# Router logits of a graph layer with the router weights as the stationary operand, four quarters of the array side by side, and a changed routing order

## The chip, the cores and the metric

The kernel runs on one core of a Trainium2 chip. The metric is the device time of one execution in microseconds (us). In this text PE is TensorE (PEld its weight loads), DVE is VectorE, ACT is ScalarE, POOL is GpSimd and SP is the queue that issues most DMAs. An fp32 product is shown in the profile as two records ("passes"); a product of the rounded type fp32r, and a transpose, as one.

## The reference, cut to what matters

Everything is float32, 384 tokens of 1024 features. A graph attention (16 heads, edge mask) and a linear attention with a gated feed-forward net are added to the input; the sum is normalised and goes through a mixture of eight experts, of which each token takes one:

```python
x = x + gnn(xn, ...) + mix(xn, ...)
t = layernorm(x)                              # 384 x 1024
logits = t @ switch_w + switch_b              # 384 x 8
route_prob = softmax(logits)
routes = argmax(route_prob)
for e in range(8):                            # w1[e] 1024 x 512, w2[e] 512 x 1024
    y = gelu(t @ w1[e] + b1[e]) @ w2[e] + b2[e]
    out = where(routes == e, y, out)
x = x + out * max(route_prob)
```

The change is in how `t @ switch_w` is formed, and in the order of what stands around it.

## The kernel before, in words

Each engine has its own program, written out in order, and they meet at semaphores. Tokens are in three tiles t of 128 rows, features in eight groups k of 128. Most matrix products are made of three fp32r products of high and low parts. The last stage before the experts goes like this:

- The output projection (`project`, L1770) adds the attention to `tok`. Its second half is done tile by tile; after a tile DVE adds it up (`projected`, L1282 to L1287) and subtracts the mean (`centred`, L1309), which gives x2[t]. POOL makes 1/sigma (`rstd`, L515).
- PE transposes x2[t] (L1791) into two PSUM banks, ACT copies them to `x2t[t]` (L856; for the third tile DVE copies one of the two, L1424), and scales x2[t] into its high part (L864 to L867, semaphore `x2_hi`). DVE then makes the low part (`split_x2`, L1297, semaphore `x2_split`).
- `logits(t)` (L1799): for each k the 128x128 block of `x2t[t]` is the stationary operand and the 8 columns of `swt` move through; 8 fp32 products, added up in PSUM. Tiles 0 and 1 come in a row, before the transposes of tile 2, which come before the logits of tile 2.
- DVE's `choices` (L1384 to L1401) finds the expert of each token as a row of zeros and a one (`hot_r`). PE counts how many tokens of each expert stand before each token (L1850 to L1852 for tiles 0 and 1, L1880 and L1881 for tile 2), and DVE's `places` (L1410 to L1417) makes of it a matrix `place[t]` of 128 tokens by 512 slots.
- `gather` (L1865): with x2's high and low parts as stationary operands and `place[t]` moving, PE sorts the tokens by expert: 8 k, 2 parts, 3 tiles, 48 fp32r products of 512 columns. ACT copies the results. Then the experts' products follow (L1917), for two experts at a time, each in one half of the array's columns, with their weights in a ring of 30 buffers that SP fills as they are read.

Of the kernel before, what the change touches and what calls it, by code (L numbers as in the profile page):

```python
# [18 lines left out]
ALU = mybir.AluOpType  # L19
ACT = mybir.ActivationFunctionType  # L20
F32 = mybir.dt.float32
F32R = mybir.dt.float32r
I32 = mybir.dt.int32
AX_X = mybir.AxisListType.X

P = 128
N = 384
NT = N // P
D = 1024
KT = D // P  # L30
# [9 lines left out]
EXPERTS = 8  # L40
# [17 lines left out]
C_EXP = C_SLOT + OVER * EXPERTS  # L58
C_IOTA = C_EXP + 1
# [17 lines left out]
EARLY = 5  # L77
# [70 lines left out]
def graph_layer(nc, x, rowb, cols, consts, later, src_rows, dst_rows, src_cols, dst_cols, type_cols,  # L148
                type_weights, w_stream, w_experts, switch_w, b12, out):
    with ExitStack() as ctx:  # L150
        def sb(name, shape, dt=F32):
            return ctx.enter_context(nc.sbuf_tensor(name, shape, dt))

        def sem(name):
            return ctx.enter_context(nc.semaphore(name))
# [24 lines left out]
        with nc.sbuf_tensor("place_ab", [P, NT * N], F32R) as place_ab:  # L180
            pass
        maskb = sb("maskb", [P, NT, N])
        with nc.sbuf_tensor("edges_a", [P, 2, N], I32) as edges_a:
            pass
        qp = sb("qp", [P, 2, N], F32R)
# [48 lines left out]
        vt = row_buf[:, 0:N]  # L234
        qp_row, kp_row = qp[:].rearrange("p a b -> p (a b)"), kp[:].rearrange("p a b -> p (a b)")
        tri_r, place_late = qp_row[:, 0:2 * P], qp_row[:, 0:NT * SLOT].rearrange("p (t n) -> p t n", t=NT)
        ident = cst[:, C_ID:C_ID + P]
        tri = cst[:, C_TRI:C_TRI + P]
        ones = cst[:, C_ONE:C_ONE + P]
# [73 lines left out]
            sem("pos_done"))  # L313
        tri_set, hots_set = sem("tri_set"), sem("hots_set")
        x2t_half = sem("x2t_half")
        place_done, got_ready, got_done = sem("place_done"), sem("got_ready"), sem("got_done")
        blk_in = [sem(f"blk_in{h}") for h in range(len(HOMES))]
        blk_read = sem("blk_read")
# [40 lines left out]
        def x2t_banks(t):  # L359

            return (3, 4) if t == 1 else (0, 2)

        def logit_bank(t):

            return 1 if t < 2 else 0
# [272 lines left out]
        def _(act):  # L638
# [220 lines left out]
            def split_x2(t):  # L859

                act.wait_ge(rstd_done, 3 * NT + t + 1)
                r = rs[:, t, 1:2]
                if t < 2:
                    nc.scalar.activation(pt_row[:, t * D:(t + 1) * D], x2[t], ACT.Identity, scale=r).then_inc(x2_hi, 1)  # L864
                else:
                    nc.scalar.activation(pt_row[:, 2 * D:2 * D + 2 * P], x2[t][:, 0:2 * P], ACT.Identity, scale=r)
                    nc.scalar.activation(vp_row, x2[t][:, 2 * P:D], ACT.Identity, scale=r).then_inc(x2_hi, 1)  # L867
# [6 lines left out]
                                         bias=rt[:, R_NMAX, t:t + 1], accum_out=rt[:, R_SUM, t:t + 1])\  # L874
                        .then_inc(lexp_done, 1)

            for t in range(NT):
                x2t_copy(t)
                split_x2(t)
            act.wait_ge(lmax_done, 1)  # L880
            exponentials(0, 2)
            act.wait_ge(lmax_done, 2)
# [38 lines left out]
        def _(dve):  # L921
# [368 lines left out]
            def split_x2(t):  # L1290

                dve.wait_ge(x2_hi, t + 1)
                dve.wait_ge(x2t_ready, t + 1)

                def rest(dst, value, hi):

                    return nc.vector.scalar_tensor_tensor(out=dst, in0=value, scalar=rs[:, t, 1:2],  # L1297
                                                          in1=hi.bitcast(F32), op0=ALU.mult, op1=ALU.subtract)

                if t < 2:  # L1300
                    rest(x2_lo[t], x2[t], pt_row[:, t * D:(t + 1) * D]).then_inc(x2_split, 1)
                else:
                    rest(x2_lo[t][:, 0:2 * P], x2[t][:, 0:2 * P], pt_row[:, 2 * D:2 * D + 2 * P])
                    rest(x2_lo[t][:, 2 * P:D], x2[t][:, 2 * P:D], vp_row).then_inc(x2_split, 1)
# [24 lines left out]
            for first in (0, 32):  # L1329
                rows = slice(first, first + EXPERTS)  # L1330
                ins = nc.vector.tensor_copy(kp_row[rows, 0:EXPERTS * SLOT].rearrange("p (s n) -> p s n", n=SLOT),
                                            slote[rows, 2, 0:EXPERTS].unsqueeze(2).to_broadcast([EXPERTS, EXPERTS, SLOT]))
            ins.then_inc(hots_set, 1)
            for b in range(HALF // P):
                nc.vector.tensor_scalar(iota[:, b * P:(b + 1) * P], cst[:, C_IOTA:C_IOTA + P], float(b * P), None,
                                        ALU.add)
# [16 lines left out]
            projected(1, 1)  # L1353
            centred(1)
            split_x2(0)
            split_x2(1)
            projected(1, 2)
            centred(2)

# [44 lines left out]
            def places(first, last, counted):  # L1404

                ts = range(first, last)
                dve.wait_ge(hot_done, counted)
                dve.wait_ge(count_ready, counted)
                for t in ts:
                    ins = nc.vector.scalar_tensor_tensor(out=of_tile(R_RANK, t), in0=count_of(t), scalar=1.0,  # L1410
                                                         in1=hot_of(t).bitcast(F32), op0=ALU.mult, op1=ALU.mult,
                                                         accum_out=seen[:, t:t + 1])
                then(ins)
                nc.vector.tensor_scalar(valid[:, first:last], seen[:, first:last], float(SLOT), None, ALU.is_lt)
                then(nc.vector.tensor_tensor(near[:, first:last], seen[:, first:last], own[:, first:last], ALU.add))
                for t in ts:
                    nc.vector.tensor_scalar(place[t], iota[:], near[:, t:t + 1], valid[:, t:t + 1],  # L1417
                                            ALU.is_equal, ALU.mult).then_inc(place_done, 1)

            dve.wait_ge(route_in, 32)  # L1420
            dve.wait_ge(logits_ready, 1)
            choices(0, 2)
            dve.wait_ge(x2t_ready, NT)
            nc.vector.tensor_copy(x2t[2][:, HALF:D], ps[:, x2t_banks(2)[1], :]).then_inc(x2t_half, 1)  # L1424
            places(0, 2, 1)
            dve.wait_ge(logits_ready, 2)
            choices(2, NT)
            places(2, NT, 2)
# [125 lines left out]
        def _(pe):  # L1554
# [239 lines left out]

            def logits(t):

                pe.wait_ge(x2t_copied, t + 1)
                for k in range(KT):
                    ins = nc.tensor.matmul(ps[:, logit_bank(t), t * EXPERTS:(t + 1) * EXPERTS],  # L1799
                                           x2t[t][:, k * P:(k + 1) * P],  # L1800
                                           swt[:, k, :], start=(k == 0), stop=(k == KT - 1))
                return ins

            pe.wait_ge(s_max, HEADS - 1)
            pe.wait_ge(out_lo, PAIRS - 2)
# [26 lines left out]
            project(1, 2, 3).then_inc(w_started, 1)  # L1832
            q_no.add(RING)

            pe.wait_ge(route_in, 32)
            logits(0)
            logits(1).then_inc(logits_ready, 1)
            transpose_x2(2)
# [11 lines left out]
            nc.tensor.matmul(count_of(0), tri_m, hot_of(0), start=True, stop=True)  # L1850
            nc.tensor.matmul(count_of(1), ones_m, hot_of(0), start=True, stop=False)
            nc.tensor.matmul(count_of(1), tri_m, hot_of(1), start=False, stop=True).then_inc(count_ready, 1)  # L1852
            pe.wait_ge(x2t_copied, NT)
            pe.wait_ge(x2t_half, 1)
            logits(2).then_inc(logits_ready, 1)

            def x2_part(part, t, k):
# [10 lines left out]
                    ins.then_inc(got_ready, 1)  # L1868

            pe.wait_ge(wo_sum, 2 * NT)  # L1870
            pe.wait_ge(x2_split, 2)
            pe.wait_ge(place_done, 2)
            for part in range(2):
                gather(0, part, 0, 2)
            for u in range(2):
                both = ps[:, 1, (NT + 2) * EXPERTS:(NT + 4) * EXPERTS].rearrange("p (t e) -> p t e", e=EXPERTS)
                nc.tensor.matmul(both, ones_m, hot_of(u).unsqueeze(1).to_broadcast([P, 2, EXPERTS]),
# [1 line left out]
            pe.wait_ge(hot_done, 2)  # L1879
            nc.tensor.matmul(count_of(2), tri_m, hot_of(2), start=False, stop=False)  # L1880
            nc.tensor.matmul(count_of(3), ones_m, hot_of(2), start=False, stop=True).then_inc(count_ready, 1)  # L1881
            for k in range(1, EARLY):
                for part in range(2):
                    gather(k, part, 0, 2)
            pe.wait_ge(x2_hi, NT)
            pe.wait_ge(place_done, NT)
            for k in range(EARLY):
# [208 lines left out]
```

## Time and profile before

| | us |
|---|---|
| median of 3 runs | 587.9 |
| lowest, highest | 587.04, 591.64 |
| profiled execution | 588.1 |
| its span, first to last instruction | 586.3 |

| engine | busy us | share of the span | instructions |
|---|---|---|---|
| PE | 557.9 | 95% | 3048 |
| PEld | 478.7 | 82% | 3048 |
| DVE | 379.5 | 65% | 743 |
| ACT | 239.0 | 41% | 387 |
| POOL | 147.1 | 25% | 161 |

Around the span lie 1.8 us in which no instruction runs. Busy time of PE counts a product that is in the array, whether it fills it or not, and at whichever of its two clocks it runs; so the share says that PE has nearly always work, not that it works at its peak. The stage that the change touches is the stretch from 483 to 507 us of the span.

### The profile page before, as it was taken

The page shows a single profiled execution, that of the slowest core. Times are in us where ns is not written, and L with a number is a line of the kernel's source. Part 1 is how long each engine was busy: PE and PEld are TensorE (multiplying, and loading weights), DVE is VectorE, ACT ScalarE, POOL GpSimd, SP SyncE. Part 2 cuts the span into 40 slices and gives each one's busy share as a digit, 9 for nine tenths or more (in the row PEclk, how much of TensorE's full clock was granted, in tenths as well). Part 3 has the DMA queues.
Part 4 walks back from the last instruction along what each step waited for, and adds up shares of the span by engine and source line. Part 5 has one row for each costly group of instructions (what it writes and reads, how often), then busy time and mean ns, then how long its engine had stood idle before and what let it go on. Part 6 is the DMA issues. An engine that isn't in the chain of part 4 may idle for free.

```text
span 586.3 us, 8511 instructions
## 1 busy us (share of the span) xinstructions
PE 557.9 (95%) x3048; PEld 478.7 (82%) x3048; DVE 379.5 (65%) x743; ACT 239.0 (41%) x387; POOL 147.1 (25%) x161
## 2 busy tenths in 40 slices
PE   3989999999999999999999999999998999999995
PEld 3989997897999999999979999999997888633321
DVE  6688887755777447673558889888979776200114
ACT  3646553410233434344326665676477321320000
POOL 5627665751176500080000001001002010000020
PEclk9999999999999999999999999999998996999998
DMA  8655657530263554448532226325459686199943
GB/s 304 212 143 193 163 175 235 148 107 1 71 190 109 187 180 140 149 148 285 149 82 103 72 72 153 98 72 143 143 182 315 248 325 266 63 387 412 411 161 110
DMA packets 33777, 104.18 MB, mean 178 GB/s; under 512 B 5424, under 2 KB 9712, under 8 KB 33744
## 3 DMA queue, kind: packets, MB, share of 16 engines
q1 hardware_dynamic: 28224, 89.95, 44.5%
q0 software_dynamic: 5376, 13.29, 8.7%
q10 hardware_dynamic: 144, 0.52, 0.3%
q8 instruction: 17, 0.28, 0.2%
q14 instruction: 16, 0.13, 0.1%
HBM read 96.58 MB, written 5.60 MB: 174 GB/s over the span
## 4 chain that ended last, share of the span: by engine, by line
PE 83%; DVE 7%; ACT 3%; DMA 2%; issue 2%; POOL 1%; DVEq 0%; SPq 0%; ACTq 0%
PE ps L1577 42%; PE ps L1917 10%; PE ps L1770 6%; PE ps L1591 5%; PE ps L1724 3%; PE ps L1714 3%; DVE wsp L933 2%; PE ps L1865 2%; PE ps L1699 2%; PE ps L1661 2%; PE ps L1642 2%; PE ps L1734 2%; DMA tw<-in_type_weights 1%; PE ps L1799 1%; DMA tok<-in_x 1%
## 5 line engine op out<-in xcount | busy, mean ns | idle before, releaser
L1577 PE MATMUL ps<-big,wsp 128*128 128x384 f32 x1656 | 295.6, 337 | 3.6 <-DVE wsp L933 2.8
L1577 PEld LDWEIGHTS ps<-big,wsp 128*128 128x128 f32 x1656 | 286.0, 188 | 8.1 <-issue 5.6
L933 DVE TENSOR_TENSOR wsp<-raw,wsp 128x1024 fp32r<-128x1024 f32 x85 | 111.0, 1311 | 30.6 <-ACT wsp L650 29.7
L650 ACT ACTIVATE wsp<-raw 128x1024 fp32r<-128x1024 f32 x83 | 87.0, 1052 | 32.9 <-PE ps L1591 12.9
L559 POOL DMA_INDIRECT edge_table<-ef,eidx x48 | 55.5, 1155 | 34.5 <-DMA edge_table<-ef,eidx 22.5
L657 ACT ACTIVATE big<-ps,bias 128x384 f32 x24 | 14.0, 582 | 80.8 <-PE ps L1577 80.8
L1917 PE MATMUL ps<-blocks 128*64 128x512 f32 x192 | 43.8, 599 | 0.0
L944 DVE SCALAR_TENSOR_TENSOR big<-ps,bias,big 128x384 f32 (+1 forms) x24 | 14.8, 617 | 34.1 <-ACT big L657 33.5
L774 ACT ACTIVATE work<-work,snm 128x384 f32<-128x384 f32 x48 | 28.9, 604 | 16.1 <-DVE snm L1200 16.1
L1591 PE MATMUL ps<-wsp,big 128*128 128x512 f32 x144 | 33.1, 391 | 0.4 <-DVE wsp L933 0.4
L1917 PEld LDWEIGHTS ps<-blocks 128*64 128x64 f32 x192 | 12.7, 136 | 23.8 <-issue 23.8
L1591 PEld LDWEIGHTS ps<-wsp,big 128*128 128x128 f32 x144 | 27.0, 188 | 6.3 <-DVE wsp L933 0.8
L596 POOL DMA_DIRECT2D tok<-rowbuf x3 | 2.8, 934 | 96.5 <-ACT tok L801 96.5
L515 POOL TENSOR_SCALAR rs<-mv 128x1 f32<-128x1 f32 x12 | 6.1, 506 | 81.7 <-DVE mv L952 47.5
L1482 DVE COPY maskb<-ps 128x512 f32<-128x512 f32 x4 | 2.8, 692 | 34.8 <-PE ps L1917 34.8
L1196 DVE CUSTOM_DVE_ANT_0 work<-ps,maskb 128x384 f32<-128x384 f32 x48 | 24.1, 553 | 1.6 <-issue 1.6
L933 DVE TENSOR_TENSOR pt<-ps,pt 128x1152 fp32r<-128x1152 f32 x16 | 21.7, 1357 | 1.4 <-ACT pt L782 1.3
L1482 DVE COPY row_buf<-ps 128x512 f32<-128x512 f32 x4 | 2.8, 691 | 30.5 <-PE ps L1917 30.5
L1009 DVE SCALAR_TENSOR_TENSOR work<-codes,ef,maskb 128x384 f32<-128x384 int32 (+2 forms) x48 | 22.1, 510 | 0.0
L1724 PE MATMUL ps<-pt,vp 128*128 128x384 f32 x96 | 20.2, 345 | 1.1 <-DVE pt L933 0.7
L1770 PE MATMUL ps<-wsp,big 128*128 128x512 f32 x72 | 18.9, 421 | 1.8 <-DVE snm L1200 1.8
L782 ACT ACTIVATE pt<-ps 128x1152 fp32r<-128x1152 f32 x16 | 18.1, 1134 | 3.7 <-PE ps L1714 3.5
(242 smaller groups left out, 722.7 us busy)
## 6 DMA issues: line engine op xcount, KB each, us to landing
raw<-in_w_stream SPq DMA_DIRECT2D x85, 512.0 KB, 3.6
blocks<-in_w_experts SPq DMA_DIRECT2D x64, 512.0 KB, 9.2
rowbuf<-in_rowb POOLq DMA_DIRECT2D x6, 512.0 KB, 6.0
raw_x<-in_w_stream SPq DMA_DIRECT2D x4, 512.0 KB, 7.3
slot_y<-rowbuf POOLq DMA_DIRECT2D x7, 256.0 KB, 5.8
tok<-in_x SPq DMA_DIRECT2D x3, 512.0 KB, 4.0
edges_a<-in_src_rows SPq DMA_DIRECT2D x8, 192.0 KB, 4.3
edges_a<-in_dst_rows SPq DMA_DIRECT2D x8, 192.0 KB, 5.4
```

Source lines behind the costliest of these rows:

```text
L559: pool.indirect_dma_start(out=table, out_offset=bass.IndirectOffsetOnAxis(ap=eidx[:, c:c + 1], axis=0), in_=ef[:, 3, c:c + 1], in_offset=N ...
L650: nc.scalar.activation(wsp[:, 0, slot, :], raw[:, slot, :], ACT.Copy).then_inc(w_hi, 1)
L774: nc.scalar.activation(probs[:, s, t, :], probs[:, s, t, :], ACT.Exp, bias=snm[:, s, t:t + 1], scale=DH ** -0.5, accum_out=ssum[:, s, t:t ...
L782: nc.scalar.activation(pt[:, 0, :, :], ps[:, b:b + 3, 0:N], ACT.Copy).then_inc(pt_hi, 1)
L933: return nc.vector.tensor_tensor(dst, value, hi.bitcast(F32), ALU.subtract)
L1009: ins = nc.vector.scalar_tensor_tensor(out=into[k], in0=codes[buf][:, k * P:N], scalar=ef[:, 0, bass.ds(c + k, 1)], in1=maskb[:, k, k * P: ...
L1196: ins = nc.vector.tensor_tensor_reduce(out=probs[:, s, t, :], in0=ps[:, 2 + 3 * s + t, 0:N], in1=maskb[:, t, :], scale=1.0, scalar=3.0 * N ...
L1577: ins = nc.tensor.matmul(ps[:, bank, 0:N], wsp[:, a, slot, k * P:(k + 1) * P], moving[:, b, k, :], start=(k == 0 and n == 0), stop=(k == K ...
L1591: ins = nc.tensor.matmul(ps[:, banks + t, :], stationary[:, b, k, t * P:(t + 1) * P], wsp[:, a, slot, kk * HALF:(kk + 1) * HALF], start=(k ...
L1724: ins = nc.tensor.matmul(ps[:, bank, 0:N], vp[:, mt, s, :], pt[:, b, mt, :], start=(mt == 0 and b == 0), stop=(mt == NT - 1 and b == 1))
L1770: ins = nc.tensor.matmul(ps[:, 2 + 3 * h + t, :], feat[0][:, b, k, t * P:(t + 1) * P], split_of(slot_of(Q_WO + h * RING + j), a)[:, kk * H ...
L1917: ins = nc.tensor.matmul(ps[s * SLOT:(s + 1) * SLOT, bank, :], stationary(k, s), rows[s][:, kk * HALF:(kk + 1) * HALF], start=False, stop= ...
```

## The change

The roles in the product are swapped. `switch_w` is spread out to 32 columns per k (8 weights, 24 zeros) in a tile `swt_wide`, which is now the stationary operand, and the 128 columns of `x2t[t]` move. Since it fills a quarter of the array's columns, four k are put side by side, each in its quarter, so that PSUM gets the four partial sums of k = g and k = 4 + g in 32 partitions each (`partial_logits`). ACT copies the 128x128 result to SBUF (`l_copy`), and one more product with a matrix `fold` (128x8, ones where the row's expert is the column) adds the four quarters and turns the result to tokens by experts (`logits`). DVE builds `swt_wide` and `fold` once, ahead of `iota`.

Around it the order changes: DVE's low part of tile 1 (`split_x2(1)`) comes after `places(0, 2)`. On ACT the copies of the logits stand after `split_x2(1)` and, for tile 2, ahead of `split_x2(2)`, behind a wait for the first logits. PE's early gathers take first the high parts of k = 0 to 4 and then the low ones, three of the high ones ahead of the counts of tile 2.

```diff
+        l_rows = [routing[:, (2 + n) * P:(3 + n) * P] for n in range(2)]
+        swt_wide = routing[:, 2 * N + 4 * P:2 * N + 6 * P].rearrange("p (k e) -> p k e", e=32)
+            def l_copy(t):
+                act.wait_ge(l_ready, t + 1)
+                nc.scalar.activation(l_rows[t % 2], ps[:, l_bank(t), 0:P], ACT.Copy).then_inc(l_copied, 1)
-            for t in range(NT):
+            for t in range(2):
                 x2t_copy(t)
                 split_x2(t)
+            for t in range(2):
+                l_copy(t)
+            x2t_copy(2)
+            act.wait_ge(logits_ready, 1)
+            l_copy(2)
+            split_x2(2)
...
+            then(nc.vector.memset(swt_wide, 0.0))
+            dve.wait_ge(route_in, 32)
+            nc.vector.tensor_copy(swt_wide[:, :, 0:EXPERTS], swt[:])
+            groups = cst[:, C_IOTA:C_IOTA + P].rearrange("p (g n) -> p g n", g=4)[:, :, 0:EXPERTS]
+            then(nc.vector.tensor_scalar(fold_of.rearrange("p (g e) -> p g e", g=4), groups, cst[:, C_EXP:C_EXP + 1],
+                                         None, ALU.is_equal))
+            nc.vector.reduce_sum(fold, fold_of.rearrange("p (g e) -> p e g", g=4), AX_X).then_inc(swt_set, 1)
...
             split_x2(0)
-            split_x2(1)
             projected(1, 2)
...
             places(0, 2, 1)
+            split_x2(1)
             dve.wait_ge(logits_ready, 2)
...
             def logits(t):
+                pe.wait_ge(l_copied, t + 1)
+                return nc.tensor.matmul(ps[:, logit_bank(t), t * EXPERTS:(t + 1) * EXPERTS], l_rows[t % 2], fold,
+                                        start=True, stop=True)
+            def partial_logits(t):
                 pe.wait_ge(x2t_copied, t + 1)
-                for k in range(KT):
-                    ins = nc.tensor.matmul(ps[:, logit_bank(t), t * EXPERTS:(t + 1) * EXPERTS],
-                                           x2t[t][:, k * P:(k + 1) * P],
-                                           swt[:, k, :], start=(k == 0), stop=(k == KT - 1))
-                return ins
+                for r in range(2):
+                    for g in range(4):
+                        k = 4 * r + g
+                        ins = nc.tensor.matmul(ps[32 * g:32 * (g + 1), l_bank(t), 0:P], swt_wide[:, k, :],
+                                               x2t[t][:, k * P:(k + 1) * P], start=(r == 0), stop=(r == 1))
+                ins.then_inc(l_ready, 1)
...
-            pe.wait_ge(route_in, 32)
+            pe.wait_ge(swt_set, 1)
+            partial_logits(0)
+            partial_logits(1)
             logits(0)
             logits(1).then_inc(logits_ready, 1)
             transpose_x2(2)
...
-            pe.wait_ge(x2t_copied, NT)
             pe.wait_ge(x2t_half, 1)
+            partial_logits(2)
             logits(2).then_inc(logits_ready, 1)
...
-            pe.wait_ge(x2_split, 2)
+            pe.wait_ge(x2_hi, 2)
             pe.wait_ge(place_done, 2)
-            for part in range(2):
-                gather(0, part, 0, 2)
+            for k in range(3):
+                gather(k, 0, 0, 2)
...
-            for k in range(1, EARLY):
-                for part in range(2):
-                    gather(k, part, 0, 2)
+            for k in range(3, EARLY):
+                gather(k, 0, 0, 2)
+            pe.wait_ge(x2_split, 2)
+            for k in range(EARLY):
+                gather(k, 1, 0, 2)
```

How PE's program reads from the logits of tile 1 to the first gather, before (a name ahead of the arrow is the PSUM tensor, behind it stand the moving and the stationary operand; the shape is that of the result):

```order
L1799 MATMUL ps<-swt,maskb 128x8 [waits x2t_copied]
L1799 MATMUL ps<-swt,maskb 128x8 x7
L1791 MATMUL ps<-cst,work 128x128 [waits x2_done]
L1791 MATMUL ps<-cst,work 128x128 x7
L1850 MATMUL ps<-hot_r,qp 128x8 [waits hot_done,tri_set]
L1851 MATMUL ps<-hot_r,qp 128x8
L1852 MATMUL ps<-hot_r,qp 128x8
L1799 MATMUL ps<-swt,row_buf 128x8 [waits x2t_copied,x2t_half]
L1799 MATMUL ps<-swt,row_buf 128x8 x7
L1865 MATMUL ps<-place_ab,pt 128x512 [waits place_done,x2_split,wo_sum]
```

And PE's program of the change at the same place (`routing` holds `swt_wide`, `l_rows` and `fold`):

```order
L1834 MATMUL ps<-maskb,routing 32x128 [waits x2t_copied]
L1834 MATMUL ps<-maskb,routing 32x128 x7
L1825 MATMUL ps<-routing 128x8 [waits l_copied] x2
L1818 MATMUL ps<-cst,work 128x128 [waits x2_done]
L1818 MATMUL ps<-cst,work 128x128 x7
L1886 MATMUL ps<-hot_r,qp 128x8 [waits hot_done,tri_set]
L1887 MATMUL ps<-hot_r,qp 128x8
L1888 MATMUL ps<-hot_r,qp 128x8
L1834 MATMUL ps<-row_buf,routing 32x128 [waits x2t_copied,x2t_half]
L1834 MATMUL ps<-row_buf,routing 32x128 x7
L1825 MATMUL ps<-routing 128x8 [waits l_copied]
L1901 MATMUL ps<-place_ab,pt 128x512 [waits place_done,x2_hi,wo_sum]
```

The groups of eight products stand where they stood (that of tile 0 is right ahead of these rows in both); behind tiles 0 and 1 come two products, behind tile 2 one, that wait for ACT's copies, and the first gather no longer waits for `x2_split`.

ACT's program in the same stretch, of the change. Before, the three rows of L890 were not there:

```order
L866 ACTIVATE maskb<-ps 128x512 [waits x2t_ready]
L866 ACTIVATE maskb<-ps 128x512
L874 ACTIVATE pt<-rowbuf,rs 128x1024 [waits rstd_done]
L890 ACTIVATE routing<-ps 128x128 [waits l_ready] x2
L866 ACTIVATE row_buf<-ps 128x512 [waits x2t_ready]
L890 ACTIVATE routing<-ps 128x128 [waits l_ready,logits_ready]
L876 ACTIVATE pt<-work,rs 128x256 [waits rstd_done]
L877 ACTIVATE vp<-work,rs 128x768
L883 ACTIVATE rt<-rt 128x8 [waits lmax_done]
```

## Rows read from the trace of the kernel before

**Rows 1.** The chain that ended last, 483 to 515: start us, us, what.
```profile
483.47 3.48 PE ps L1799 x32
...
487.04 0.37 DVE rt L1384 x2
...
488.82 0.35 PE ps L1850
...
489.38 0.21 PE ps L1852
489.59 3.42 PE ps L1799 x16
493.01 1.91 PE ps L1865 x4
...
495.57 11.27 PE ps L1865 x44
...
507.16 0.23 PE ps L1925
507.39 7.02 PE ps L1917 x32
514.41 0.44 PE ps L1925
```

**Rows 2.** Windows, PE alone: us, PE busy (x), PEclk, DMA share, GB/s.
```profile
443.50:444.00 0.50, 0.50 (x2) 0.50 1.01 385
...
446.50:447.00 0.50, 0.50 (x3) 0.82 1.05 426
...
487.60:487.80 0.20, 0.20 (x3) 0.61 1.07 430
...
497.80:498.00 0.20, 0.20 (x2) 0.79 0.00 0
```

**Rows 3.** Timeline of PE: start, us, line, op, out<-in, count [idle before <-releaser].
```profile
442.92 5.98 PE L1770 MATMUL ps<-wsp,big 128*128 128x512 f32 x18 [1.83 <-DVE snm L1200]
```

**Rows 4.** Timeline of DVE, 456 to 495.
```profile
456.77 0.70 DVE L1319 MEMSET kp<- 128x768 f32 x1
...
466.82 0.69 DVE L1282 TENSOR_TENSOR tok<-tok,ps 128x512 f32<-128x512 f32 x1 [1.13 <-PE ps L1770]
...
482.91 1.28 DVE L1297 SCALAR_TENSOR_TENSOR x_lo_ab<-rowbuf,rs,pt 128x1024 fp32r<-128x1024 f32 x1 [2.35 <-ACT pt L864]
484.11 0.68 DVE L1282 TENSOR_TENSOR tok<-tok,ps 128x512 f32<-128x512 f32 x1
...
485.80 0.75 DVE L1309 TENSOR_SCALAR work<-tok,mv 128x1024 f32<-128x1024 f32 x1
487.04 0.36 DVE L1384 SCALAR_TENSOR_TENSOR rt<-ps,rs,sbias 128x8 f32<-128x8 f32 x2 [0.49 <-PE ps L1799]
...
488.65 0.68 DVE L1424 COPY row_buf<-ps 128x512 f32<-128x512 f32 x1
489.71 0.17 DVE L1410 SCALAR_TENSOR_TENSOR rt<-ps,hot_r 128x8 f32<-128x8 f32 x1 [0.37 <-PE ps L1852]
...
490.27 1.00 DVE L1417 TENSOR_SCALAR place_ab<-iota,rt 128x512 fp32r<-128x512 f32 x2
493.05 0.23 DVE L1384 SCALAR_TENSOR_TENSOR rt<-ps,rs,sbias 128x8 f32<-128x8 f32 x1 [1.78 <-PE ps L1799]
...
494.03 0.23 DVE L1398 TENSOR_SCALAR hot_r<-rt 128x8 fp32r<-128x8 f32 x1
```

**Rows 5.** Timeline of ACT, 461 to 490.
```profile
461.30 0.49 ACT L790 ACTIVATE low_rows<-ps 64x384 f32<-64x384 f32 x1 [3.14 <-PE ps L1724]
...
488.00 0.60 ACT L856 ACTIVATE row_buf<-ps 128x512 f32<-128x512 f32 x1 [5.13 <-PE ps L1791]
...
489.72 0.29 ACT L873 ACTIVATE rt<-rt 128x8 f32<-128x8 f32 x1
```

**Rows 6.** Timeline of PE, 571 to 575.
```profile
571.45 2.84 PE L1958 MATMUL ps<-row_buf,iota 128*128 128x512 f32 x6
```

More of the change, by code:

```diff
@@ L182, in graph_layer @@
         maskb = sb("maskb", [P, NT, N])
+        with nc.sbuf_tensor("routing", [P, 4 * N], F32) as routing:
+            pass
         with nc.sbuf_tensor("edges_a", [P, 2, N], I32) as edges_a:
@@ L236, in graph_layer @@
         tri_r, place_late = qp_row[:, 0:2 * P], qp_row[:, 0:NT * SLOT].rearrange("p (t n) -> p t n", t=NT)
+        l_rows = [routing[:, (2 + n) * P:(3 + n) * P] for n in range(2)]
+        fold_of, fold = routing[:, 4 * P:4 * P + 4 * EXPERTS], routing[:, 4 * P + 4 * EXPERTS:4 * P + 5 * EXPERTS]
+        swt_wide = routing[:, 2 * N + 4 * P:2 * N + 6 * P].rearrange("p (k e) -> p k e", e=32)
         ident = cst[:, C_ID:C_ID + P]
@@ L315, in graph_layer @@
         x2t_half = sem("x2t_half")
+        swt_set, l_ready, l_copied = sem("swt_set"), sem("l_ready"), sem("l_copied")
         place_done, got_ready, got_done = sem("place_done"), sem("got_ready"), sem("got_done")
@@ L361, in x2t_banks, with l_bank @@
             return (3, 4) if t == 1 else (0, 2)
+        def l_bank(t):
+            return 4 if t == 1 else 2
         def logit_bank(t):
@@ L1418, in places @@
                                             ALU.is_equal, ALU.mult).then_inc(place_done, 1)
-            dve.wait_ge(route_in, 32)
             dve.wait_ge(logits_ready, 1)
```

## The prediction

> **What bounds the kernel now.** I first read the shares of busy time: PE has work in 95% of the span, so a gain must shorten what PE does or how long it waits. Then the chain of waits around the change [rows 1]. It runs from the projection into the logits of tiles 0 and 1 (483.47, 3.48 us), over DVE's choice of experts (487.04) to PE's counts (488.82), through the logits of tile 2 (489.59, 3.42 us) into the gathers (493.01 to 506.84) and straight on into the experts' products. So the whole stretch is on the path, and what the gathers' end moves, the end of the kernel moves: behind it the view of waits shows none of PE on a load, and the later loads are released by PE's own reading. Last I read the granted clock [rows 2]. It is at 2.4 GHz up to 487.68 (0.61 over 0.2 us), at 1.2 GHz until 497.88 (0.79), and 2.4 GHz again. It had done the same before: 1.2 GHz by 443.5, back at 446.68 (0.82 over 0.5 us). That is why sixteen passes of logits take 3.42 us for tile 2 and only 1.74 us each for tiles 0 and 1.
>
> Gathering at full clock is 11.4 us of work: 4.87 us at half clock (493.01 to 497.88) count as 2.43, and 8.96 us follow.
>
> **The change, part by part.**
>
> *The products.* A logits pass of before takes 3.48/32 = 0.109 us though only 8 columns move; its stationary operand is 128 wide. Of the new passes (the same number, two for each of eight products) each moves 128 columns against 32 stationary ones. No row shows such a pass. The nearest are the experts' products, two halves side by side: 7.02/32 = 0.219 us a pass of 512 columns [rows 1], where the same type across the full array takes 2.84/6 = 0.47 [rows 6]. So there the array does two at once. A quarter of the columns moved gives 0.219/4 = 0.055 us a pass. That is also what I take with four quarters: the two passes of one product need the same quarter and must follow each other, and if products start in order, only the second pass of one and the first of the next can overlap, however many quarters there are. The ends are 0.027 (all four at once) and 0.109 (nothing overlaps). Going from full width to parts of the array and back costs a little: a full product behind full ones takes 0.23 us in the chain, behind halves 0.44 [rows 1], so 0.21 us each time. There are two such trips, and I double that at half clock.
>
> The Trainium skill, "TensorE: Matmul & The Clock Gate", Part 1, has a rule against this: if the sequencer's microcode decodes them, matmuls come no faster than one in about 62 ns. The closest passes in my rows are these 0.109 us apart, so no run here shows whether it holds; with 0.062 the first 32 passes would take 0.2 us more and the result would be an estimated 0.2 us later.
>
> *The copy.* ACT has nothing to do between its work for tile 1 (done at 482.9) and 488.00 [rows 5]. A copy of 64x384 from PSUM takes 0.49 us, 128x512 0.60, and the smallest operation 0.29; so 128x128 is between 0.29 and 0.49, and I take 0.30, since by the first two 128 columns cost 0.11 and 128 instead of 384 leave 0.27. The copy of tile 0 lies under the passes of tile 1; that of tile 1 is on the path, with some 0.05 us for each hand-over.
>
> *The folding product.* Two passes behind a wait: as for L1850 and L1852, 0.35 and 0.21 at half clock [rows 1], I take 0.25 + 0.11 at full clock and 0.1 for the hand-over.
>
> *Tiles 0 and 1.* 483.47 + 0.21 + 32 x 0.055 = 485.44; copy done 485.8; logits at 486.25; DVE starts at 486.3. Before it started at 487.04: 0.7 us earlier. DVE itself must be free: its chain `projected` to `centred` of tile 2 ran from 484.11 to 486.55, held up by the low part of tile 1 that started at 482.91 and took 1.28 [rows 4]. That low part is moved away, so the chain starts at 483.55, ends at 486.0, and is no wait, nor is it one for the transposes of tile 2, which follow at 486.25. Without this move DVE would still be busy until 486.55, and the gain would be 0.5.
>
> *Tile 2.* The counts come 0.7 us earlier, at 488.12, and end at 488.89. DVE's half copy of x2t (488.65 to 489.33) moves along and is in time. Passes at half clock: 2 x 0.21 + 16 x 0.11 = 2.18 gives 491.07; ACT's copy, for which only a wait for the first logits stands ahead, 491.45; folding 0.1 + 0.35 + 0.21 gives 492.1. Before: 493.01. So the gathers can begin 0.9 us earlier.
>
> *What stands behind the new waits.* On ACT the high part of tile 2 now waits for that copy and starts at 491.45; it and the low part are wanted only behind the 20 early gathers, which alone take over 4.5 us. On DVE `places(0, 2)` starts at 489.0 (0.7 before 489.71) and ends at 490.57; then comes the low part of tile 1, 1.28 us, until 491.85, and the logits of tile 2 at 492.15 are not kept waiting. The margin is 0.3 us: with quicker logits DVE becomes the next wait. The new order of the gathers covers the 1.2 us in which DVE chooses for tile 2 (493.05 to 494.2 before): at half clock six products of 1.91/4 = 0.48 us [rows 1]. The gathers' number is the same, 48.
>
> *Setting up.* Four DVE operations ahead of `iota`: a fill of 128x256 (0.70 us for 128x768, so 0.25) and three small ones, together about 0.9 us. They are covered by 1.13 us in which DVE waited for PE at 466.82 [rows 4]; if they overran, 2.35 us of waiting at 482.91 would take it. No DMA, SP or POOL instruction is moved.
>
> *The clock.* Gathers from 492.1 run at half clock until it comes back. In the first stall the dense products began at 442.92 [rows 3] and the clock rose 3.76 us later; in the second the gathers began at 493.01 and it rose 4.87 later. I take the middle, 4.3 us: at 496.4, 2.15 of the 11.4 us are done, and 9.25 remain: 505.65 instead of 506.84, 1.2 us earlier. The ends 3.76 and 4.87 give 1.5 and 0.9.
>
> The sum is against the profiled execution: 588.1 - 1.2 = 586.9. That execution is 0.2 above the median of the runs, 587.9; I make no correction for it.
>
> **The rivals.**
>
> *The clock comes back in the middle of this.* The new passes move 128 columns, not 8. If they count as dense work, the 3.76 to 4.87 us run from 489.1, and the clock rises near 493.4. The gathers have then done 0.65 us and need 10.75 more: 504.15, a gain of 2.7, 585.4. For it speaks that the fall at 487.68 came after 3.4 us of nearly nothing but 8-column products and transposes; against it the waits that now stand between the groups.
>
> *All four quarters at once.* 0.027 us a pass saves 0.9 us in the first 32 passes and 0.9 in the next 16: a further 1.8, 585.1. The Trainium skill, "TensorEngine Tiling (Array Packing)", Overview, gives up to 4x for 32 columns. The halves' two-fold overlap agrees with that rule and with products starting in order alike.
>
> *The clock never falls.* Then the logits of tile 2 would be there at 490.6, but DVE is in the low part of tile 1 until 491.8 and chooses until 493.0; PE stands for 0.8 us behind its three early gathers. It ends at 502.9: 584.2. Idle PE time grows with the change, which speaks against it.
>
> *Slower: the passes do not overlap in quarters.* The one mechanism is the spacing of the 32-column passes. At 0.109 us nothing is saved in the products, and copies, folding products and trips come on top: DVE starts at 488.0 instead of 487.04, the counts end at 490.5, the 16 passes take 3.9 us, the gathers begin at 495.5. They end at 509.05, 2.2 us later: 590.3. It decides from a spacing of about 0.074 (64 units of spacing, counting tile 2 double, for 1.2 us). The halves speak against it; that only halves, never quarters, are seen here speaks for it.
>
> *No gain to be seen.* Hand-overs and trips cost 0.3 us more each time and eat it: 588.0.
>
> **How the numbers follow.** Forecast 0.38, clock back early 0.20, four at once 0.08, never falls 0.04, no gain 0.13, slower 0.17. The predicted time is the likeliest case's, 586.9. The range 584.8 to 589.3 takes in the first three and no gain, and of the slower case the spacings up to about 0.09; 584.2 and the full 590.3 are out, some 0.18. A measurement of this kernel tells 1%, 5.9 us, from no change; every case is within it, so 0.95 for the same, 0.02 for faster and 0.03 for slower, for something not thought of.
>
> **What would show it.** Passes of L1834 0.055 us apart at full clock, the 32 done in 1.8 us; DVE's L1411 at 486.3 with its wait ended by PE; the first gather (L1901) at 492.1, no idle time of PE in the gathers; clock back near 496.4; last gather at 505.65. Wrong would be a wait of PE for `l_copied` over 1 us, a wait of DVE's choice for its own low part, or passes over 0.07 us.

## The result and the profile after

| | before | changed |
|---|---|---|
| median us (6 runs each) | 588.44 | 584.76 |
| lowest, highest | 587.04, 591.64 | 583.66, 585.36 |
| profiled execution, its span | 588.1, 586.3 | 584.88, 583.2 |

The ratio is 0.9929, 95% interval 0.9904 to 0.9954: 3.7 us faster, where 1.2 were forecast, and just below the range's low end of 584.8. Measured again later (experiment 5) it gave 0.9963 (0.9945 to 0.9982). By the two pairs of medians the gain is 3.7 and 2.3 us; the two intervals overlap only just.

The chain of waits of the changed kernel through the same stretch (start us, us, what), which answers to [rows 1]:

```profile
480.81 2.77 PE ps L1797 x12
483.58 0.02 issue
483.61 0.70 DVE tok L1303
484.31 0.02 issue
484.33 0.70 DVE stats L1305
...
485.97 0.36 DVE rt L1411 x2
...
487.67 0.60 DVE row_buf L1450
488.27 0.04 issue
488.32 1.12 PE ps L1834 x16
...
489.52 0.29 ACT routing L890
489.81 0.04 issue
489.85 0.60 PE ps L1825 x2
490.45 2.76 PE ps L1901 x6
...
493.86 10.27 PE ps L1901 x42
```

The logits of tiles 0 and 1 are gone from the chain: from the last product of the projection it goes over DVE's own statistics to its first choice, at 485.97. Then it goes over DVE's half copy of x2t (487.67) to the logits of tile 2. The first gather starts at 490.45 where it started at 493.01, and the last ends at 504.13, not 506.84: 2.7 of the 3.1 us between the spans. The other 0.4 us lies behind DVE's last sum, which also comes 2.7 us earlier (575.47, before 578.15); only the output stands there, and the change does not touch it.

The timeline of PE (start, us, line, op, what, count [idle before <-releaser]):

```profile
483.50 0.64 PE L1834 MATMUL ps<-work,routing 128*32 128x128 f32 x16
483.96 0.62 PE L1834 MATMUL ps<-maskb,routing 128*32 128x128 f32 x16
484.54 0.82 PE L1825 MATMUL ps<-routing 128*128 128x8 f32 x4
486.11 1.09 PE L1818 MATMUL ps<-cst,work 128*128 128x128 f32 x8 [0.74 <-DVE work L1330]
487.75 0.24 PE L1886 MATMUL ps<-hot_r,qp 128*128 128x8 f32 x1 [0.54 <-DVE hot_r L1425]
```

Sixteen passes take 483.96 - 483.50 = 0.46 us, 0.029 a pass, about a quarter of the 0.109 of before. PE has more idle time than before, not less: 0.74 us ahead of the transposes, 0.54 ahead of the counts. Before, it ran without a gap from the logits (483.31) to the end of the transposes and then waited 0.85 us for DVE's choice.

The granted clock (windows of PE: us, PE busy, PEclk, DMA share, GB/s), which answers to [rows 2]:

```profile
488.00:488.20 0.20, 0.20 (x2) 0.99 1.00 410
488.20:488.40 0.20, 0.10 (x5) 0.50 0.92 348
...
494.80:495.00 0.20, 0.20 (x2) 0.50 0.00 0
495.00:495.20 0.20, 0.20 (x2) 0.94 0.00 0
```

At 1.2 GHz from 488.2 to 495.0, 6.8 us, where it was 10.2 us (487.64 to 497.88; the 487.68 of the prediction is a slip in reading 0.61 over 0.2 us).

### The profile page after: what moved, and what is told of

Its sections match the earlier page's. It is cut to its first block, busy times and chain, and to the rows that moved or that the text cites. A ratio compares the mean times of both kernels' runs of the same rounds, so it can differ in the third digit from the quotient of the medians.

```text
span 583.2 us, 8532 instructions
## 1 busy us (share of the span) xinstructions
PE 554.5 (95%) x3054; PEld 473.9 (81%) x3054; DVE 381.9 (65%) x747; ACT 240.0 (41%) x390; POOL 148.4 (25%) x161
## 4 chain that ended last, share of the span: by engine, by line
PE 80%; DVE 11%; ACT 4%; issue 3%; DMA 1%; POOL 0%; DVEq 0%; SPq 0%; ACTq 0%
PE ps L1604 41%; PE ps L1955 10%; PE ps L1797 6%; PE ps L1618 5%; DVE wsp L954 4%; PE ps L1901 2%; PE ps L1741 2%; PE ps L1751 2%; PE ps L1726 2%; PE ps L1688 2%; PE ps L1669 2%; PE ps L1761 2%; ACT wsp L660 1%; DMA tok<-in_x 1%; DVE big L954 1%
## 5 line engine op out<-in xcount | busy, mean ns | idle before, releaser
L1797 PE MATMUL ps<-wsp,big 128*128 128x512 f32 x72 | 18.9, 420 | 1.8 <-DVE snm L1221 1.8
L1227 DVE TENSOR_SCALAR work<-work,sinv 128x384 f32<-128x384 f32 x48 | 19.3, 460 | 0.6
```

The lines of the kernel that those rows point to most:

```text
L1227: ins = nc.vector.tensor_scalar(probs[:, s, t, :], probs[:, s, t, :], sinv[:, s, t:t + 1], None, ALU.mult)
L1797: ins = nc.tensor.matmul(ps[:, 2 + 3 * h + t, :], feat[0][:, b, k, t * P:(t + 1) * P], split_of(slot_of(Q_WO + h * RING + j), a)[:, kk * H ...
```

## The experiments

Each was timed in five rounds or more against the kernel before on its own chip. Experiments 1 to 4 and 9 to 12 ran on one chip, 5 to 8 on another, so ratios may be compared across the two groups, times only with care. The mean clock is that of all executions of a kernel, over the whole span, not of the profiled one alone. "Half clock" is what the profiled execution shows between 484 and 500 us; "to the end" is the time on PE from the first logits product to the transposes behind the gathers (L1897 before, 23.36 us; 20.47 in the change), so it leaves out how late PE gets there.

| | kernel | median us | ratio (interval) | mean clock | half clock us | to the end us |
|---|---|---|---|---|---|---|
| | before, with 1 to 4 | 588.17 | | 0.985 | 10.2 | 23.4 |
| | the change, first time | 584.76 | 0.9929 (0.9904-0.9954) | 0.990 | 6.8 | 20.5 |
| 1 | order only | 587.97 | 0.9994 (0.9973-1.0014) | 0.986 | 10.2 | 23.3 |
| 2 | swap only | 586.64 | 0.9969 (0.9945-0.9992) | 0.987 | 10.2 | 22.2 |
| 3 | two quarters | 583.74 | 0.9917 (0.9888-0.9947) | 0.994 | 0 | 18.9 |
| 4 | one quarter | 586.19 | 0.9954 (0.9931-0.9978) | 0.993 | 0 | 21.0 |
| 5 | the change again | 586.35 | 0.9963 (0.9945-0.9982) | 0.987 | 6.8 | 20.5 |
| 6 | 9 fillers | 584.18 | 0.9923 (0.9897-0.9949) | 0.993 | 0 | 18.7 |
| 7 | 18 fillers | 584.81 | 0.9928 (0.9905-0.9952) | 0.994 | 0 | 19.4 |
| 8 | before, 5 fillers | 588.78 | 1.0005 (0.9985-1.0026) | 0.985 | 10.2 | 23.6 |
| 9 | before, 128 columns moved | 585.68 | 0.9944 (0.9921-0.9966) | 0.993 | 0 | 19.9 |
| 10 | low part later | 585.19 | 0.9943 (0.9924-0.9962) | 0.988 | 6.8 | 20.4 |
| 11 | low part later, 9 fillers | 583.23 | 0.9895 (0.9872-0.9918) | 0.994 | 0 | 18.0 |
| 12 | two quarters, later, 7 fillers | 584.35 | 0.9915 (0.9888-0.9942) | 0.992 | 0 | 18.4 |

The median of before was 588.61 with 5 to 8 and 589.4 with 9 to 12, its mean clock 0.985 and 0.984. Theory "passes" says that the gain is the time of the logits' passes; its rivals give it to the order, or to the clock.

**1. Order only.** The logits stay; `split_x2(1)` and the gathers are moved.

```diff
             split_x2(0)
-            split_x2(1)
             projected(1, 2)
...
             places(0, 2, 1)
+            split_x2(1)
```

> The logits as before, only the order changed: DVE's low part of tile 1 behind places(0, 2), and the gathers with the high parts first. Theory 'passes' (the gain comes from the quicker logits): the logits of tiles 0 and 1 still end on PE at 486.95, DVE is ready half a us earlier for nothing, and the low part (until about 492.6) is done before the logits of tile 2 (493.0): same time as before, within 0.5 us. Theory 'order' (the moved low part alone frees the path): 1 us or more of the 3.1 us between the two spans appears here.

Nothing to be seen, as "passes" said: 0.9994, with an interval of 0.2 to 0.3% on either side. Half clock lasts 10.2 us as before.

**2. Swap only.** The same edit the other way round, on the change.

> The new logits with the old order on DVE and in the gathers. Theory 'passes': DVE's low part of tile 1 again stands ahead of projected(1, 2), so DVE's first choice starts at about 486.6 instead of 485.97, which costs 0.6 us; 2.5 us of the 3.1 remain, span near 583.8. Theory 'order': little remains, span 585 or more.

The mechanism came as written. In its chain of waits (start, us, what) the low part is back, with ACT's high part ahead of it:

```profile
482.02 1.05 ACT pt L874
483.07 0.02 issue
483.09 1.29 DVE x_lo_ab L1318
484.38 0.61 DVE tok L1303
...
486.65 0.37 DVE rt L1412 x2
```

DVE's first choice is 3.07 us behind the first logits product (483.58), 2.47 in the change. But the median gain is 1.5 us, not 2.5 of 3.1: half clock lasts 10.2 us here again. So neither theory has the size; the order is worth 0.6 us on the path once the logits are quick. The stretch to the gathers' end is 1.8 us longer than in the change (22.2 and 20.5), so 1.2 us are lost behind DVE's first choice; 3.4 us more at half clock can account for up to 1.7. Why half clock lasts longer here is not shown.

**3 and 4. Two quarters, one quarter.** The same eight products, two or eight k to a quarter:

```diff
-                for r in range(2):
-                    for g in range(4):
-                        k = 4 * r + g
+                for r in range(4):
+                    for g in range(2):
+                        k = 2 * r + g
```

> Only two quarters of the array are used (even k in the first, odd k in the second, four products added up in each); copy and folding product are over 64 partitions. Theory 'spacing by quarters' (as many passes run at once as there are quarters in use): 0.055 us a pass, 32 passes in 1.75 us, DVE's first choice waits for PE until about 486.2, tile 2 takes 0.055 to 0.11 a pass; the gathers begin near 491.8; span near 584.8. Rival 'narrow is quick' (a pass is quick since only 32 columns are loaded): 0.03 us a pass and the span of the change, 583.2.

> All eight k go through the first quarter of the array, one sum over eight; copy and folding product are over 32 partitions. Theory 'spacing by quarters': 0.109 us a pass as in the logits of before, 3.5 us for the 32, DVE's first choice near 487.9, tile 2 at half clock 3.5 us, the gathers begin near 494.5; about 1.5 to 2 us slower than before. Rival 'narrow is quick': 0.03 to 0.06 us a pass and faster than before.

The spacing is as "spacing by quarters" said. Two quarters (timeline of PE):

```profile
485.34 1.07 PE L1834 MATMUL ps<-work,routing 128*32 128x128 f32 x16
486.24 1.04 PE L1834 MATMUL ps<-maskb,routing 128*32 128x128 f32 x16
```

One quarter:

```profile
485.13 1.93 PE L1832 MATMUL ps<-work,routing 128*32 128x128 f32 x16
486.90 1.91 PE L1832 MATMUL ps<-maskb,routing 128*32 128x128 f32 x16
```

0.90/16 = 0.056 us and 1.77/16 = 0.111 us a pass. That refutes "narrow is quick", though the span that this rival gave for two quarters, 583.2, is the one measured: a coincidence, since the passes took 0.056 us and not 0.03. The times refute what "spacing by quarters" made of its spacing. By their medians two quarters are no slower than four, and one quarter, whose passes are no quicker than those of before and which has the copies on top, is faster than before by 0.46%. The clock accounts for it (windows of PE; two quarters, then one):

```profile
484.00:488.00 4.00, 3.95 (x44) 1.00 0.98 316
488.00:492.00 4.00, 2.67 (x29) 1.00 0.95 384
492.00:496.00 4.00, 3.64 (x18) 1.00 1.00 404
```

```profile
484.00:488.00 4.00, 4.00 (x33) 1.00 0.92 325
488.00:492.00 4.00, 3.06 (x24) 1.00 1.02 417
492.00:496.00 4.00, 3.58 (x24) 1.00 0.85 344
```

It does not fall in this stretch at all. The same windows of the kernel before:

```profile
484.00:488.00 4.00, 3.96 (x35) 0.96 0.94 342
488.00:492.00 4.00, 3.18 (x15) 0.50 1.03 422
492.00:496.00 4.00, 4.00 (x15) 0.50 0.48 190
```

PE was as busy before the fall (3.96 of 4 us) as where there was none. So here the busy column does not foretell it.

**5. The change again.**

> The changed kernel again, beside the fillers. All theories: 0.993 of before, within 0.002. The theory that the clock's fall and rise lie where they lie by chance expects its profile to show the half clock from another moment than 488.2 and for 3.4 to 7 us; the rival, that they follow the program, 488.2 to 495.0 again within 0.3 us.

0.9963, beyond the 0.002 allowed. In its profile half clock lasts 6.8 us again, but from 490.3, where PE's first logits product comes at 485.10, 1.6 us later than in the first profile. So the fall follows that product by 5.2 us here and by 4.7 us there: not the same moment within 0.3 us, and two profiles do not tell whether it comes by chance. The path is the same: 20.54 and 20.47 us to the end of the gathers. What differs lies ahead of the stage that was changed. Windows of PE from 130 to 140 us of the span, in this profile and then in the first:

```profile
130.00:140.00 10.00, 8.83 (x40) 0.83 0.01 2
```

```profile
130.00:140.00 10.00, 8.83 (x48) 1.00 0.01 2
```

A clock of 0.83 over 10 us is 3.4 us at half clock, which can cost up to 1.7 us, and the stage starts 1.6 us later. The mean clock is 0.987 here and 0.990 in the first measurement. The profiles of 3, 4, 7, 8, 11 and 12 have such a stretch between 30 and 40 us, that of 9 has one at either place, and in all of them the stage starts 1.3 to 2.3 us later than before; the profiles of before, of the change and of 1, 2, 6 and 10 have none in the first 200 us. This is why the last column counts from the first logits product. What brings such a stretch on is not known.

**6 and 7. Fillers.** fp32r products of 384 columns into a free bank, in PE's idle places: 4, 3 and 2, or 8, 6 and 4.

```diff
+            def fill(n):
+                for i in range(n):
+                    nc.tensor.matmul(ps[:, 5, 0:N], feat[0][:, 0, i % KT, 0:P], feat[0][:, 0, i % KT, :],
+                                     start=True, stop=True)
...
             logits(1).then_inc(logits_ready, 1)
+            fill(4)
             transpose_x2(2)
+            fill(3)
...
             partial_logits(2)
+            fill(2)
```

> The changed kernel with 9 more fp32r products of 384 columns, results not used, in PE's idle places: 4 behind the logits of tile 1, 3 behind the transposes of tile 2, 2 behind the partial logits of tile 2. They cost nothing by themselves where they fit into 0.7, 0.5 and 0.4 us of idle time (0.165 us each). Theory 'idle PE lets the clock fall': half clock is shorter or gone, up to 2.5 us faster than the change. Rival 'the clock falls anyway': same as the change, or 0.3 slower.

> As the run with 9 fillers, with 18 (8, 6, 4), more than fits: 1.5 us of products that delay the path by 0.2 to 0.7 us. Theory 'idle PE lets the clock fall': no half clock at all in this stretch, 2 us faster than the change though it does more. Rival: 1 to 1.5 us slower than the change.

With 9 fillers the clock holds between 484 and 500 us, and to the end it takes 18.7 us instead of 20.5; with 18 it holds too and takes 19.4. "Idle PE lets the clock fall" had the direction right; but the fillers also are products of 384 columns, so whether the filled gap or the columns moved held the clock is not separated. In medians 9 fillers gain 2.2 us over experiment 5, on the same chip (584.18 and 586.35), and 0.6 over the first measurement. The mean clock of their six executions is 0.989 to 0.996, that of the twelve of experiment 5 is 0.982 to 0.989. A new wait shows in the timeline of 6:

```profile
491.30 0.28 PE L1922 MATMUL ps<-hot_r,qp 128*128 128x16 f32 x2
492.07 0.27 PE L1925 MATMUL ps<-hot_r,qp 128*128 128x8 f32 x1 [0.48 <-DVE hot_r L1425]
```

That is the wait priced in the rival "the clock never falls": the gathers are too quick to cover DVE's choice, which stands behind the low part.

**8. Before with fillers.** `fill(5)` behind the transposes of tile 2.

> The kernel before with 5 such products behind the transposes of tile 2, where PE waited 0.85 us. Theory 'idle PE lets the clock fall': the fall at 487.7 is later or gone and some of the 2.4 us of lost work (half of 4.9) come back; rival 'the 8-column products let it fall': no change, since these stand before and after.

1.0005: no change, and half clock lasts 10.2 us again. But the test is weaker than it was meant to be, as its timeline of PE shows:

```profile
486.34 1.93 PE L1805 MATMUL ps<-swt,maskb 128*128 128x8 f32 x16
488.13 1.07 PE L1791 MATMUL ps<-cst,work 128*128 128x128 f32 x8
488.95 1.84 PE L1798 MATMUL ps<-big 128*128 128x384 f32 x5
```

The fillers start at 488.95 and the clock falls at 489.1, and in the kernel before the filled gap (488.0 to 488.8) lies behind the fall at 487.64. So they could hardly have prevented the fall; what they show is that work in this gap does not bring the clock back sooner. That idle time was not what let it fall follows from the timeline of before itself: PE had no gap between 483.31 and the fall.

**9. Before, 128 columns moved.** The one that decides. The weights are read sixteen times over. The wider results need room, so they go to PSUM banks 5 and 2 (before: 1 and 0), and DVE reads its 8 columns there; order, waits and the number of products are those of before.

```diff
-                    ins = nc.tensor.matmul(ps[:, logit_bank(t), t * EXPERTS:(t + 1) * EXPERTS],
-                                           x2t[t][:, k * P:(k + 1) * P],
-                                           swt[:, k, :], start=(k == 0), stop=(k == KT - 1))
+                    out_l = ps[:, 5 if t < 2 else 2, t * P:(t + 1) * P].rearrange("p (c e) -> p c e", e=EXPERTS)
+                    ins = nc.tensor.matmul(out_l, x2t[t][:, k * P:(k + 1) * P],
+                                           swt[:, k, :].unsqueeze(1).to_broadcast([P, P // EXPERTS, EXPERTS]),
+                                           start=(k == 0), stop=(k == KT - 1))
```

> The kernel before, but the 8 columns of the router weights move sixteen times over in each product (128 columns, 16 copies of the logits, of which DVE reads the first). The stationary operand, the number of passes and the order stay. Theory 'the passes are bound by their 128-wide weight load and the clock falls since so little moves': 0.109 us a pass as before at full clock, the 2.4 GHz clock holds through the logits, tile 2 takes 1.8 us in place of 3.4 and the gathers run at full clock; up to 4 us faster than before, 584 to 586. Rival 'the clock falls because PE waits': half clock for 10 us again, same time as before.

0.9944, 3.7 us under the median of before, with sixteen times the columns. Its timeline and its windows:

```profile
485.59 1.95 PE L1800 MATMUL ps<-swt,work 128*128 128x128 f32 x16
487.38 1.95 PE L1800 MATMUL ps<-swt,maskb 128*128 128x128 f32 x16
...
491.81 2.02 PE L1800 MATMUL ps<-swt,row_buf 128*128 128x128 f32 x16
493.59 0.71 PE L1866 MATMUL ps<-place_ab,pt 128*128 128x512 f32 x2
```

```profile
488.00:492.00 4.00, 2.85 (x25) 1.00 0.97 382
492.00:496.00 4.00, 3.75 (x27) 1.00 0.99 404
```

A pass takes 1.79/16 = 0.112 us, as with 8 columns, so the passes are not quicker; the clock stays at 2.4 GHz between 484 and 500 us, the logits of tile 2 take 1.8 us where they took 3.4, and the gathers start at full clock. It is not the luck of one profile: the mean clock of all six executions is 0.990 to 0.996, that of the seventeen of before beside them 0.981 to 0.986. The means, 0.9932 and 0.9841, differ by 0.0091; over 586 us this is 5.3 us at full clock, or some 10.7 us at half clock, as an estimate, and the profile of before has 10.2 in this stretch. This edit alone brings, within the intervals, what the change brings. The other banks are not tested apart; no pass got quicker and no wait shorter by them, so the columns are the likelier cause.

**10, 11 and 12. The low part later.** `split_x2(1)` behind `choices(2)`: on the change, with the 9 fillers, and with two quarters and 7 fillers (2, 3, 2).

```diff
             places(0, 2, 1)
-            split_x2(1)
             dve.wait_ge(logits_ready, 2)
             choices(2, NT)
+            split_x2(1)
```

> The changed kernel with DVE's low part of tile 1 behind choices(2) instead of ahead of it. Theory: while the clock is low the six early gathers cover the choice, so nothing is gained then; where the clock stays up, up to 0.5 us. Expected ratio 0.994 to 0.997, within 0.5 us of the change.

> The same with the 9 fillers of e6. Theory 'clock': as e6 half clock is mostly gone, and then DVE's choice for tile 2, for which PE stood 0.48 us in e6, is no longer waited for: 0.4 us faster than e6, ratio 0.991 to 0.992. Rival: the low part is then wanted by PE in turn (x2_split) and the 0.48 us come back there.

> Two quarters in place of four, low part of tile 1 behind choices(2), 7 fillers (2, 3, 2). Theory 'clock': the slower passes of the two quarters cost 0.1 us at DVE's first choice and keep the array in work longer; half clock in no run or few, ratio 0.990 to 0.991, 583. Rival: the fillers add nothing to what e3 had (0.9917).

10 is not to be told from either measurement of the change. 11 has the lowest ratio of all, 0.9895, 6.2 us under before and below the 0.991 to 0.992 expected; its interval overlaps that of 6 (0.9897 to 0.9949). Its PE no longer waits for DVE's choice, and the low part is not waited for in turn:

```profile
493.14 0.28 PE L1922 MATMUL ps<-hot_r,qp 128*128 128x16 f32 x2
493.28 0.25 PE L1925 MATMUL ps<-hot_r,qp 128*128 128x8 f32 x1
```

It beats the kernel before. Against the change its interval lies below that of experiment 5 (taken on the other chip) and overlaps that of the first measurement. 12, with 0.9915 where 0.990 to 0.991 was expected, is not to be told from 3 (0.9917) or 11; its rival, that fillers add nothing to two quarters, stands.

## Why the prediction was wrong

*What failed first: the spacing of the passes.* I took 0.055 us, on the ground that products start in order and only neighbours overlap. It is 0.029, close to the end of 0.027 that I had priced as the rival "all four quarters at once". That rival was given 0.08. Its mechanism is the one measured, and its time is near: a gain of 3.0 us, 585.1, where the profiled execution took 584.88. Its split is not: it had 0.9 us from the first 32 passes and 0.9 from the next 16, and they gave 0.3 and 1.1. That the sum fits so well is in part luck, since the path gives 2.7 us and the output behind it 0.4. The rows before could not decide it, since halves overlap alike by both rules; experiments 3 and 4 show that as many passes run at once as there are quarters in use. "TensorEngine Tiling (Array Packing)" of the Trainium skill, Overview, gives up to 4x for 32 columns, and the trace agrees: 0.109 to 0.029 is 3.8x. The floor of 62 ns that I weighed from the Trainium skill, "TensorE: Matmul & The Clock Gate", Part 1, is stated there for matmuls decoded by microcode; with passes 0.029 us apart it does not bind here.

*Where it went.* The first gather starts 1.65 us before the forecast (490.45, forecast 492.1). For tiles 0 and 1 little of it was gained: the passes end 0.9 us before the forecast, but DVE's own chain sets its first choice (485.97, forecast 486.3), so 0.3 us is left. Some 0.25 us comes from there to the passes of tile 2: the clock fell at 488.2 and not at 487.7, so the counts ran 0.11 us apart instead of 0.21, and DVE's half copy, which I had called in time, became the wait ahead of the passes. For tile 2 the spacing counts in full: 1.12 us for trip and passes, forecast 2.18, so 1.1 us. Of the 1.65 us the last gather keeps 1.5 (504.13, forecast 505.65), as the clock rose 4.6 us behind the first gather and not 4.3.

*What failed beneath: the clock as a given.* I let it fall at 487.7 in every case but one of 0.04, and looked for what shortened the path. In the profiled execution that did little harm, as the clock rose between my 3.76 and 4.87 us behind the first gather in the chain. But experiment 3 has just the spacing that I forecast, and its profile ends the stretch at 18.9 us, because the clock holds, where my working gave some 22.2 (483.47 to 505.65). Experiment 9 gains as much without any quicker pass. Against the rival "the clock never falls" I had held that the change adds idle time. That is half of it: the change as it is does lose the clock, and with fillers in its idle places it does not (6, 7). But in the kernel before there was no idle time ahead of the fall. There stood a row of 8-column products, 4.2 us from its start to the fall, the last 0.7 of them transposes, and with 128 columns in their place the clock did not fall (9). I had named that row in the rival "the clock comes back in the middle of this", and gave it the wrong consequence: the time of the fall, not whether there is one.

*What was right.* The path itself and its order of waits; the trip into quarters, small (with all of this profile 0.1 us later, the first pass starts 0.19 us later than the first of before, so 0.09); the copy, 0.28 us (forecast 0.30); the folding product, 0.60 us at half clock (forecast 0.56); the moved low part, no gain by itself (1), 0.6 us with quick logits (2); the setting up on DVE, hidden; the early gathers covering DVE's choice at half clock; and the wait that takes their place when the clock is high (0.48 us in 6, where I had priced 0.8).

*What stays open.* The spread between executions goes with the clock (mean clock and time of the 29 executions of before that go with 1 to 4 correlate with -0.90), but what decides in one execution whether it falls was not found, nor why half clock lasts 6.8 us in the change and 10.2 in experiment 2. That the change gained less the second time goes with half clock ahead of the stage in the one profile there is (5); for the other executions it is not shown. So the change's gain can't be split for good: in these profiles 2.9 us are gained up to the gathers' end, counted from the first logits product, of which half clock shortened by 3.4 us is at most 1.7.

## What to carry to other kernels

Before a run of narrow products on a busy engine, ask not only what they cost but at what clock the work behind them will run: the granted clock in small windows shows it; the busy share did not here. Turning a product round, so that the wide side moves, can pay twice, by the passes side by side and by the clock behind them. Here a pass took as long with 8 as with 128 columns moved, and moving more paid by itself. When an experiment fills a gap, check first that the gap lies ahead of what it is to prevent: in experiment 8 it did not. When a path gets shorter, look at once for what stands in the queue of the engine behind it: here the order of two DVE operations gave nothing alone and was worth something only with the rest.

## What the runs showed of the hardware

- Narrow stationary operands in different quarters of the array: 0.111 us a pass in one quarter, 0.056 in two, 0.029 in four, all at 2.4 GHz with 128 columns moved in fp32.
- The time of a pass with a 128-wide fp32 stationary operand is nearly the same with 8 and with 128 columns moved (0.109 and 0.112 us), but in the profiles the clock fell behind the first and held behind the second.
- A clock of 1.2 GHz comes in stretches outside the stage as well, and not in every execution: at 443 to 447 us in the profile of before and not in those of experiments 1 and 9, at 130 to 140 us in that of 5 and not in the first of the change. Each lasted 3.4 us.
- The granted clock varies between executions of one program (before: 0.981 to 0.989), and with it the time: the five executions at 0.981 that go with experiments 1 to 4 took 590.9 to 592.1 us, the five at 0.989 took 586.7 to 588.1. "TensorE: Matmul & The Clock Gate" of the Trainium skill, Part 1, says that the gate follows how busy the array has lately been. By the profile's busy column the traces here do not agree: PE was busy for 3.96 of the 4 us in which the clock fell before, and for 4.00 of the same 4 in experiment 9, where it did not fall.
